# Attention in groups of four heads, with the softmax division moved to the output stage

## The reference

```
q, k, v = x@Wq.T, x@Wk.T, x@Wv.T      # 32 query heads, 8 key/value heads, 128 features per head
q, k = rope(rmsnorm(q)), rope(rmsnorm(k))
k_all = concat(k_cache[block_table], k)   # 16 pages of 32 keys = 512 cached keys, then 32 new ones
v_all = concat(v_cache[block_table], v)
scores = q @ k_all.T / sqrt(128); cached keys beyond cache_seqlens are masked
x = x + (softmax(scores) @ v_all) @ Wo.T
```

## Time and profile before

| | us |
|---|---|
| three runs | 1394.37, 1390.13, 1393.95 (median 1393.95) |
| the profiled execution | 1388.88 |
| its span in the trace | 1387.2 |
| first to last `values` product of attention (L993) | 459.9 to 1178.4 |
| last instruction of the output stage's TensorE work | about 1384 |

### The profile page before, as it was taken

One profiled execution on the slowest core, in us unless ns is written; L12 is line 12 of the kernel. 1 busy time (PEld: TensorE's weight loads), 2 busy tenths in 40 slices (PEclk: granted clock), 3 DMA queues, 4 the chain that ended last, 5 costly groups with the idle time before them and its releaser, 6 DMA issues. The chain is left out here.

```text
span 1387.2 us, 30173 instructions
## 1 busy us (share of the span) xinstructions
PE 1308.6 (94%) x8584; PEld 1134.9 (82%) x8584; DVE 924.2 (67%) x2550; ACT 750.8 (54%) x1825; POOL 743.7 (54%) x737
## 2 busy tenths in 40 slices
PE   4987999999995999999999999999999999489999
PEld 3734888888885899999999999989999998378887
DVE  4695677777764777777777777777777776432222
ACT  2074444444433677777777777767777776431121
POOL 2031999999996665656666656656566663000000
PEclk9998999999997799999999999999999999789999
DMA  9203344444338988989888988878898881643341
GB/s 302 99 32 121 79 128 125 129 132 125 80 98 222 279 246 241 255 234 263 227 263 233 252 237 244 252 222 250 241 257 232 256 235 53 238 140 115 119 130 60
DMA packets 256499, 258.26 MB, mean 186 GB/s; under 512 B 57509, under 2 KB 218021, under 8 KB 256454
## 3 DMA queue, kind: packets, MB, share of 16 engines
q1 hardware_dynamic: 246406, 232.46, 58.3%
q0 software_dynamic: 9472, 25.21, 6.6%
q10 hardware_dynamic: 576, 0.05, 0.1%
HBM read 211.49 MB, written 46.14 MB: 186 GB/s over the span
## 5 line engine op out<-in xcount | busy, mean ns | idle before, releaser
L1048 DVE CUSTOM_DVE_ANT_1 att_neg<-att_mask,att_ps 128x576 f32<-128x576 f32 x256 | 193.1, 754 | 151.8 <-PE att_ps L95 151.8
L941 POOL TENSOR_TENSOR att_k_lo<-att_kT,att_k_hi 128x544 fp32r<-128x544 f32 x128 | 173.5, 1355 | 140.8 <-ACT att_k_hi L1150 140.7
L941 POOL TENSOR_TENSOR att_k_lo<-all_room_a,att_k_hi 128x544 fp32r<-128x544 f32 x128 | 174.1, 1362 | 134.9 <-ACT att_k_hi L1150 134.9
L1135 ACT ACTIVATE att_prob<-att_neg,att_nmax 128x544 f32<-128x544 f32 x256 | 191.5, 748 | 28.9 <-DVE att_nmax L1048 6.1
L1141 ACT ACTIVATE att_pT<-att_pb 128x256 f32<-128x256 f32 x256 | 98.1, 383 | 180.5 <-PE att_pb L981 180.5
L93 PE MATMUL prj_ps<-prj_wt_hi,early_xT_lo 128*128 128x512 f32 (+1 forms) x512 | 180.2, 352 | 8.2 <-DVE prj_wt_lo L732 8.2
L93 PE MATMUL att_ps<-att_k_hi,att_q_lo 128*128 128x288 f32 (+1 forms) x512 | 171.3, 335 | 10.7 <-POOL att_k_lo L941 10.6
L94 PE MATMUL prj_ps<-prj_wt_lo,early_xT_hi 128*128 128x512 f32 (+1 forms) x512 | 174.8, 341 | 0.0
L95 PE MATMUL prj_ps<-prj_wt_hi,early_xT_hi 128*128 128x512 f32 (+1 forms) x512 | 173.2, 338 | 0.0
L94 PE MATMUL att_ps<-att_k_lo,att_q_hi 128*128 128x288 f32 (+1 forms) x512 | 149.0, 291 | 0.0
L95 PE MATMUL att_ps<-att_k_hi,att_q_hi 128*128 128x288 f32 (+1 forms) x512 | 149.0, 291 | 0.0
(11 more groups left out here) (146 smaller groups left out, 3356.0 us busy)
## 6 DMA issues: line engine op xcount, KB each, us to landing
all_room_a<-in_k_cache_t SPq DMA_DIRECT2D x256, 128.0 KB, 3.9
att_kT<-in_k_cache_t SPq DMA_DIRECT2D x256, 128.0 KB, 3.5
all_room_b<-in_L_cond_v_cache SPq DMA_DIRECT2D x160, 128.0 KB, 3.1
att_vc<-in_L_cond_v_cache SPq DMA_DIRECT2D x160, 128.0 KB, 3.1
q_scratch<-prj_qst SPq DMA_DIRECT2D x64, 256.0 KB, 2.2
o_scratch<-att_ost SPq DMA_DIRECT2D x32, 512.0 KB, 4.6
out_o_n<-o_scratch SPq DMA_DIRECT2D x32, 512.0 KB, 3.5
all_room_b<-in_L_cond_v_cache POOLq DMA_DIRECT2D x96, 128.0 KB, 3.9
```

The source lines that it names most:

```text
L941: g.tensor_tensor(k_lo[j % SPLITS][:], kT[j // HK % 2][:, :, j % HK, :], f32(k_hi[j % SPLITS][:]), ALU.subtract).then_inc(k_split, 1)
L1048: v.tensor_tensor_reduce(halves[0], halves[1], ps[j % 2][:, :, 0:KA], 1.0, 3.0e38, ALU.add, ALU.min, nmax[j % 2][:]).then_inc(maxed, 1)
L1135: act.activation(prob[j % 2][:], neg[j % 2][:, 0:KEYS], ACT.Exp, bias=nmax[j % 2][:, 0:1], scale=-1.0, accum_out=total[j % 2][:]).then_inc ...
```

## The change

- The probabilities stay undivided. The sums of 8 heads are collected in `total`, one reciprocal per batch goes into a table `inv`, which is transposed at the end of the stage and stored to `inv_d`. The output stage loads for each unit the 128 x 1024 factors it needs (`partition_broadcast` reads the same 4 KB for each of 128 partitions) and GpSimd multiplies `o_n` by them before ACT rounds it.
- The new keys' probabilities of four heads are gathered side by side (`pn`, 128 x 128), transposed in one go (`turn_new`), and copied by ACT as four diagonal blocks of 32 keys x 128 queries into a zeroed tile `pnT` (128 x 4 x 128). One float32 product of 512 columns with the dense new values `vd` (128 x 128) per group, `new_values`, takes the place of four products over 32 rows.
- `turn` does four transposes into one bank (`pt`), and DVE copies all 512 columns in one instruction (`keep`). ACT copies no more than the new keys' blocks.
- q is split four heads at a time. `valued` is raised once for four heads.
- The scratch tensors and value tiles have another order: a q load is 2 DMAs with 2 KB runs in place of one with 512 B runs, value pages come in runs of 2 KB in place of 4 KB, and `ost` is stored in 2 DMAs of 2 KB runs in place of one of 4 KB runs. The new values come in 512 B runs in place of 4 KB.

The diff, cut to its core:

```diff
...
 def load_new_keys(eng, q_d, k_d, b, q, tile, sem):
-    eng.dma_start(q[:], q_d[bass.ds(b, 1)].rearrange("a h d x -> d (a h) x")).then_inc(sem, 16)
+    for g in range(HK // GROUP):
+        h = slice(g * GROUP, (g + 1) * GROUP)
+        eng.dma_start(q[:, h, :], q_d[bass.ds(b, 1), :, h, :].rearrange("a d h x -> (a d) h x")).then_inc(sem, 16)
     eng.dma_start(tile[:, NPP].rearrange("p h t -> p (h t)"), k_d[bass.ds(b, 1)].rearrange("a d x -> (a d) x")).then_inc(sem, 16)
...
     r = slice(j % PPT * PS, (j % PPT + 1) * PS)
-    eng.dma_start(tile[r, j // PPT, :], v_pages[bass.ds(page, 1)].rearrange("a s c -> (a s) c")).then_inc(sem, 16)
+    src = v_pages[bass.ds(page, 1)].rearrange("a s (g x) -> (a s) g x", g=HK // GROUP)
+    eng.dma_start(tile[r, :, j // PPT, :], src).then_inc(sem, 16)
...
+            eng.dma_start(vd[slot][:], v_d[bass.ds(b, 1)].rearrange("a (g h) s d -> (a h s) g d", g=HK // GROUP)
+                          ).then_inc(v_in[slot], 16)
...
+                def store_out(b, slot, g):
+                    sp.wait_ge(o_staged, b * (HK // GROUP) + g + 3)
+                    cols = slice(g * GROUP * P, (g + 1) * GROUP * P)
+                    sp.dma_start(o_d[bass.ds(b, 1), :, cols].rearrange("a d x -> (a d) x"),
+                                 ost[slot][:, g * GROUP:(g + 1) * GROUP, :].rearrange("p h x -> p (h x)")
+                                 ).then_inc(o_stored[slot * (HK // GROUP) + g], 16)
...
                             load_keys(sp, b + 2, slot, pages)
+                        store_out(b, slot, 0)
+                        if not tail:
                             sp.wait_ge(valued, (b + 1) * HK)
                             load_values(sp, b + 2, slot, pages)
-                        sp.wait_ge(o_staged, (b + 1) * (HK // GROUP) + 2)
-                        sp.dma_start(o_d[bass.ds(b, 1)].rearrange("a d x -> (a d) x"),
-                                     ost[slot][:].rearrange("p h x -> p (h x)")).then_inc(o_stored[slot], 16)
+                        store_out(b, slot, 1)
...
+                for half in range(2):
+                    sp.wait_ge(inv_kept, half + 1)
+                    sp.dma_start(inv_d[half * P:(half + 1) * P, :], invT[:, half, :]).then_inc(inv_stored, 16)
+                sp.wait_ge(inv_stored, 32)
+                for i in range(UNROLL // GROUP):
+                    sp.wait_ge(o_stored[i], (B // 2 + 1) * 16)
...
+                def turn(j, bank):
+                    p = prob[j // GROUP % 2][:, j % GROUP, :]
+                    for c in range(NCH):
+                        t = pe.transpose(bank[:, c * P:(c + 1) * P], p[:, c * P:(c + 1) * P], ident[:])
+                    t.then_inc(turned, 1)
+                def turn_new(j, group, bank):
+                    pe.wait_ge(gathered, group + 1)
+                    pe.transpose(bank[:, 0:P], pn[j // GROUP % 2][:].rearrange("p h t -> p (h t)"), ident[:]).then_inc(new_turned, 1)
+                def turn_inv(half, bank):
+                    pe.wait_ge(inverted, (half + 1) * B // 2)
+                    pe.transpose(bank[:, P:2 * P], inv[:, half * P:(half + 1) * P], ident[:]).then_inc(inv_turned, 1)
...
                     s, h = j // HK % 2, j % HK
-                    cols = slice(h * D, (h + 1) * D)
+                    cols = slice(h % GROUP * D, (h % GROUP + 1) * D)
                     o = po[j // GROUP % 2][:, j % GROUP * P:(j % GROUP + 1) * P]
-                    pe.wait_ge(out_b, n + 1)
-                    for c in range(NA, NCH):
-                        pe.matmul(o, vc[s][:, c, cols], pT[j % 2][:, c, :], start=(c == NA), stop=False)
-                    pe.matmul(o, vn[s][:, cols], pT[j % 2][0:S, NCH, :], start=False, stop=False)
-                    pe.wait_ge(out_a, n + 1)
-                    for c in range(NA):
-                        t = pe.matmul(o, vc[s][:, c, cols], pT[j % 2][:, c, :], start=False, stop=(c == NA - 1))
-                    t.then_inc(valued, 1)
+                    pe.wait_ge(kept, n + 1)
+                    for c in range(NCH):
+                        pe.matmul(o, vc[s][:, h // GROUP, c, cols], pT[j % 2][:, c, :], start=(c == 0 and j % GROUP == 0), stop=False)
+                def new_values(j, group):
+                    s, g = j // HK % 2, j // GROUP % 2
+                    pe.wait_ge(new_kept, group + 1)
+                    pe.matmul(po[g][:], vd[s][:, g, :], pnT[g][:].rearrange("p h q -> p (h q)"), start=False,
+                              stop=True).then_inc(valued, GROUP)
...
                     if not (tail and j + AHEAD >= UNROLL):
                         pe.wait_ge(maxed, n + 3)
-                        scores(j + AHEAD, n + AHEAD)
-                    if not (tail and j + 2 >= UNROLL):
-                        pe.wait_ge(normed, n + 3)
-                        pe.wait_ge(out_a, n + 2)
-                        pe.wait_ge(out_b, n + 2)
-                        turn(j + 2)
+                        scores(j + AHEAD, n + AHEAD, group + 1)
+                    if j % GROUP == GROUP - 2:
+                        pe.wait_ge(kept, n + 1)
+                        turn_new(j, group, pt[new_bank_of(j)])
+                        if tail and j + 1 in INV_AT:
+                            turn_inv(INV_AT.index(j + 1), pt[new_bank_of(j)])
+                    if j % GROUP == GROUP - 1:
+                        new_values(j, group)
+                    if not late:
+                        x = j + 2
+                        pe.wait_ge(exped, n + 3)
+                        if x % GROUP == 0:
+                            pe.wait_ge(kept, n + 2)
+                        elif x % GROUP == 1:
+                            pe.wait_ge(new_kept, group + 1)
+                        else:
+                            pe.wait_ge(kept, n + 1)
+                        turn(x, pt[bank_of(x)])
...
+                    if not isinstance(group, int) or group >= 2:
+                        dve.wait_ge(scored, (group - 1) * GROUP)
+                    if g * GROUP % HK == 0:
+                        dve.wait_ge(kq_in[g * GROUP // HK % 2], (it + g * GROUP // UNROLL + 1) * 16 * KQ_LOADS)
+                    src, hi, lo = q_part(g, it)
+                    v.tensor_copy(hi[:], src).then_inc(q_hi_done, 1)
+                def split_q_lo(g, it, group):
+                    dve.wait_ge(q_hi_done, group + 1)
+                    src, hi, lo = q_part(g, it)
+                    v.tensor_tensor(lo[:], src, f32(hi[:]), ALU.subtract).then_inc(q_split, GROUP)
...
                     dve.wait_ge(scored, n + 1)
+                    if not isinstance(n, int) or n >= 2:
+                        dve.wait_ge(exped, n - 1)
...
-                def normalize(j, n):
+                def gather(j, n):
                     dve.wait_ge(exped, n + 1)
-                    v.reciprocal(inv[j % 2][:], total[j % 2][:]).then_inc(inverted, 1)
-                    dve.wait_ge(inverted, n + 1)
-                    v.tensor_scalar(prob[j % 2][:], prob[j % 2][:], inv[j % 2][:, 0:1], None, ALU.mult).then_inc(normed, 1)
+                    v.tensor_copy(pn[j // GROUP % 2][:], prob[j // GROUP % 2][:, :, L:KEYS]).then_inc(gathered, 1)
+                def invert(j, n, b):
+                    s = j // HK % 2
+                    dve.wait_ge(exped, n + 1)
+                    v.reciprocal(inv[:, bass.ds(b * HK, HK)], total[s][:]).then_inc(inverted, 1)
...
-                    dve.wait_ge(turned_a, n + 1)
-                    v.tensor_copy(pT[j % 2][:, 0:NA, :], pa[:, 0:NA * P].rearrange("p (c q) -> p c q", c=NA)).then_inc(out_a, 1)
...
+                    dve.wait_ge(turned, n + 1)
+                    v.tensor_copy(pT[j % 2][:], pt[bank_of(j)][:].rearrange("p (c q) -> p c q", c=NCH)).then_inc(kept, 1)
...
+                    n, g = it * UNROLL + j, j // GROUP + 2
+                    group = it * (UNROLL // GROUP) + g
                     if not (tail and j + 3 >= UNROLL):
                         minimum(j + 3, n + 3, it * 2 + (j + 3) // HK)
                     if not (tail and j + 1 >= UNROLL):
                         keep(j + 1, n + 1)
-                    if not (tail and j + 2 >= UNROLL):
-                        normalize(j + 2, n + 2)
-                    if not (tail and j + EARLY >= UNROLL):
-                        split_q(j + EARLY, n + EARLY, it)
+                    if not (tail and g >= UNROLL // GROUP):
+                        if j % GROUP == 0:
+                            split_q_hi(g, it, group)
+                        if j % GROUP == 2:
+                            split_q_lo(g, it, group)
+                    if j % GROUP == 1:
+                        gather(j + 2, n + 2)
+                    if j % HK == HK - 3:
+                        invert(j + 2, n + 2, it * 2 + j // HK)
...
+                def exps(j, n, b, group):
+                    s, h = j // HK % 2, j % HK
+                    if j % GROUP == 0 and (not isinstance(group, int) or group >= 2):
```

(35 more changed lines are left out.)

168 lines of the change are left out of this document (79 added, 89 removed).

## The result

| | before | after |
|---|---|---|
| median of the runs, us | 1393.54 (4 runs) | 1329.28 (4 runs, lowest 1328.01) |
| ratio, 95% interval | | 0.954 [0.952, 0.956] |
| profiled execution / span, us | 1388.88 / 1387.2 | 1328.01 / 1326.3 |
| first to last value product of attention (before L992 to L996, after L1035 to L1040) | 458.8 to 1179.2 | 461.9 to 1111.5 |
| from there to the end of the span | 208.0 | 214.8 |

One of the four runs after took 1354 us, disturbed; the comparisons leave it out. The medians gain 64 us where 79 were forecast, the profiled executions 61 where the prediction's sum has 77. Of these, attention gains 71 (86 forecast, 100 less 14). Given back are 7 behind it (9 forecast, 2 and 7) and 3 before its first value product (none forecast).

A forecast was written before the change was run, and what follows sets the result against it. TensorE bounds the kernel before, and SyncE's issuing was to set attention's pace after. Profiled 1388.9 - 100 (TensorE) + 14 (SyncE) + 2 + 7 (ends) = 1312, plus 3 for the median: 1315, range 1291 to 1348.

The forecast's parts named there:

- 100 less 14: Attention: 100 us gained by TensorE's shorter heads over 256 heads, less 14 us because SyncE sets the pace.
- TensorE's head, 2.80 to 2.41 us: Attention on TensorE: fewer transposes and no 32-row products cut each head by 0.39 us, 100 us over 256 heads.
- SyncE sets the pace at 19.9 us: Attention's DMA issues: SyncE's batch grows from 18.9 to 19.9 us, over TensorE's 19.3; price +14 us (0 to +45).
- lower bound: SyncE's batch in attention: fewer q runs free the slow key-page issues, about 1 us goes, 18.8, TensorE stays the bound.
- B: Rival, attention: SyncE has room after all, slow issues gone, the 14 us fall away, 1301; chance 0.27.
- DMA priced at 0: Attention's transfers: same 5.5 MB a batch at 276 GB/s, and halving the runs of V and o costs nothing.
- E: Rival, attention's DMA: 2 KB packets cost nearly as much as 4 KB ones, kernel 1510 at 0.17 us each; chance 0.04.
- C: Rival: crowding, DMA engines (full at 280 GB/s) or the output stage's loop bind, about 1340; chance 0.17.
- The covers: Attention: DVE, ACT and POOL stay under TensorE's head, and new waits for copies and valued are priced at 0.
- The output stage: Steady units stay at 5.44 us; factor load and 2.56 us multiplication are hidden with 0.7 us to spare.
- The ends: Attention's last group +2 us; output stage's first units +7 us (3 to 12) for unhidden multiplications and loads.
- D: Rival, TensorE around L993: long steps are waits for pT, not the 32 rows; about 1378; chance 0.05.

The follow-up runs named there:

- e4_before_128: Kernel before, with the product of the 32 new values run over all 128 rows, the added rows zeroed once: 1328.14 us, ratio 0.958.
- g4_pairs: Kernel after, with GpSimd issuing its six value pages in pairs at three heads instead of one at each of six: 1329.33 us, ratio 0.958.
- f1_act_stores: Kernel after, with the two stores of ost per batch issued by ACT's queue instead of SyncE: 1332.84 us, ratio 0.960.
- f3_two_pages_less: f1_act_stores without two of SyncE's ten value pages per batch from the third batch on: 1330.37 us, ratio 0.958.
- e1_v_one_run: Kernel after, with value pages and their tile back in one run of 4 KB per partition: 1321.47 us, ratio 0.951.
- g1_act_pairs: f1_act_stores with GpSimd's six value pages issued in pairs at three heads: 1302.26 us, ratio 0.938.
- g3_less_pairs: f3_two_pages_less with GpSimd's six value pages issued in pairs at three heads: 1287.77 us, ratio 0.926.
- e5_no_factor_load: Kernel after, without the output stage's broadcast load of inv, GpSimd's multiplication kept: 1331.05 us, ratio 0.958.
- g2_one_run_pairs: Kernel after, with value pages in one 4 KB run, ost stores issued by ACT and GpSimd's value pages in pairs: 1298.45 us, ratio 0.933.
- e2_pool_8: Kernel after, with eight value pages per batch issued by GpSimd instead of six: 1445.46 us, ratio 1.041.
- e3_before_v2: Kernel before, with value pages and tiles in two runs of 2 KB: 1402.25 us, ratio 1.009.

## Why the prediction was right, and where it was off

- **TensorE's head, 2.80 to 2.41 us.** Right in kind: the cost sat around the product of 32 rows, e4_before_128 shows it alone. Slightly too dear in size: where nothing else limits, the batch is 18.7 us, 2.34 a head, since eight value passes take 0.81 us instead of 0.88. The Trainium skill (TensorEngine Tiling (Array Packing), Key Properties) says that a change of tiling mode drains TensorE; the trace agrees for the product over 32 rows (0.38 us a head, around and in it) and shows none for the transpose to 32 columns, whose steps stay at 0.11 us in e4_before_128 too.
- **SyncE sets the pace at 19.9 us.** The mechanism was right: its waits fell to 2.6 us. The term was mis-sized. The added q load and store cost 0.34 and 0.40 us and 0.30 of register work, 1.04 where 1.0 was reckoned. The step that failed is the one that changed the runs of V and priced only the packets: the issue of a value page grew from 0.37 to 0.57 us, 2.0 us a batch, which the prediction did not have. Cheaper key pages (0.8) and page numbers (0.7) gave 1.5 back, and new k 0.2. The prediction's lower bound had the gain in the key pages, but with another reason: the long issues went with the 4 KB value pages, not with q's runs. The page numbers it did not have at all. The result is 20.3 instead of 19.9. That it came so near is luck in part, since the two terms that were missed nearly cancel. Over the 29 looped batches the measured 20.46 is 16 us more than 19.9, which is the 15 us that attention missed.
- **The wait that was not seen.** The prediction names no wait for GpSimd's pages. But one page per head is a date counted in heads: with shorter heads the last one leaves 3.7 us before TensorE's need in place of 5.0, and in the denser traffic it lands after 4.7 us in place of 3.5. Each of the two takes about half of what was lost. The margin of 1.5 us before was in the trace. In the kernel after this costs nothing beyond SyncE's 20.3 (g4_pairs), but it would have kept B, "SyncE has room, 1301", from coming true: f1_act_stores gave SyncE its room and stayed at 1332.84. B needed both.
- **DMA priced at 0.** Right up to this pace: share 0.92 at 270 GB/s, and f3_two_pages_less gains nothing. E is refuted, as after moves 270 GB/s at 0.92 and e1_v_one_run with 4 KB packets 272 at 0.96; a 2 KB packet takes 0.107 us on the mean between 600 and 1050 us, under the 0.12 that the prediction set as E's sign. C's figure for full engines, 280 GB/s, is met by g1_act_pairs at 283; this limit shows only once the other two are gone.
- **The covers.** The new waits that were priced at 0 cost next to nothing: in g3_less_pairs, which has them all, TensorE is idle for 3.4 of 450 us. DVE's copy of 512 columns takes 687 ns (forecast 0.70), GpSimd's multiplication 2415 ns (2.56):

```profile
L1155 DVE COPY att_pT<-att_pt 128x512 f32<-128x512 f32 x256 | 175.8, 687 | 25.1 <-PE att_pt L1016 25.1
...
L1404 POOL TENSOR_TENSOR out_o_n<-out_o_n,all_room_b 128x1024 f32<-128x1024 f32 x32 | 77.3, 2415 | 138.0 <-DMA all_room_b<-inv_scratch 138.0
```

- **The output stage.** TensorE's step stays at 5.44 us a unit (26 of 28 steps within 0.03 us, the other two 5.57 and 5.70), and the factor's load is hidden (e5_no_factor_load). The page's DMA issues (KB each, us from issue to landing):

```profile
out_o_n<-o_scratch SPq DMA_DIRECT2D x32, 512.0 KB, 3.4
all_room_b<-inv_scratch SPq DMA_DIRECT2D x32, 512.0 KB, 5.5
```

  The second load lands 5.5 us after its issue where the sum has 4.7 (3.4 + 1.3), so by that sum nearly nothing of the 0.7 us to spare is left. The two longer steps fit that, and so do ACT's starts, which came every 5.4 to 5.5 us before and now vary from 4.6 to 6.4. The ends cost 7 us where 9 were forecast. The 3 us before attention's first value product were in no term; for 1.9 us of them TensorE stands idle until a value page has landed (0.3 before).
- **D** is refuted by e4_before_128.

## What to carry to other kernels

When a bound engine is made faster, list every piece of work that is scheduled by counting its steps, and compare lead time with latency anew: a load issued n steps ahead has fewer microseconds ahead of it afterwards, and if the traffic grows denser it may also take longer to land. When two resources end at nearly the same pace, removing either shows nothing; test them together before calling one innocent. The cost of a DMA for the engine that issues it depends on its access pattern, so a change of runs has to be priced on the queue as well as in the packets.

## What the runs showed of the hardware

- **Issue time by shape.** A load of 128 KB into 32 partitions takes SyncE 0.37 us with one run per partition (before, e1_v_one_run, g2_one_run_pairs; 244 to 285 GB/s) and 0.57 with two (e2_pool_8, e3_before_v2, after, g1_act_pairs; 230 to 283 GB/s). These are medians.
- **4 KB runs hold the issuing engine up.** With value pages of 4 KB 16 key pages take 6.7 to 7.4 us a batch, and between 600 and 1050 us 11 to 35 issues are over 0.7 us, the longest 1.6 (e4_before_128); with 2 KB the pages take 6.3 to 6.4 us and none or one issue is over 0.7 us (the longest 1.25, g4_pairs). The traffic is not the reason: g2_one_run_pairs (4 KB) and g1_act_pairs (2 KB) move 285 and 283 GB/s.
- **Reading the page numbers.** The 16 numbers that SyncE reads into registers take 2.0 to 2.1 us behind a store of 512 KB that it issued (before, e3_before_v2, e4_before_128), 1.4 to 1.5 behind one of 256 KB (after, e1_v_one_run, e2_pool_8, g4_pairs), and 1.0 where ACT issues the stores.
- **DVE and GpSimd stand in each other's way.** In g4_pairs DVE's rounding of q takes 0.42 us at best and 2.65 us where GpSimd has two instructions back to back behind its pair of DMAs (start us, us):

```profile
820.53 2.65 DVE L1123 CAST att_q_hi<-all_q 128x512 fp32r<-128x512 f32 x1
```

```profile
819.14 1.08 POOL L543 DMA_DIRECT2D all_room_b<-in_L_cond_v_cache  x2
820.25 2.64 POOL L975 TENSOR_TENSOR att_k_lo<-all_room_a,att_k_hi 128x544 fp32r<-128x544 f32 x2
```

DVE's instruction begins 0.3 us after GpSimd's first and ends 0.3 after its second. DVE's busy time in 450 us rises from 320.7 to 370.6 us with as many instructions. The Trainium skill (SBUF — State Buffer, SBUF: two separate sides) describes a port pair shared by the two, which whichever starts first holds for its whole instruction while the other is blocked. The trace agrees, with a delay that here lasts over two instructions of the other engine; no run shows that it is this port. It cost nothing here, where SyncE set the pace. In g3_less_pairs, with the same pairs, DVE is busy for 396.6 of 450 us and TensorE for 446.6; whether it costs g1_act_pairs something was not tried.
- **Granted clock.** In the kernel after TensorE idles for 29 of 450 us, in pieces of at most 2.7 us, and the mean clock stays at 0.99: twice it is 1.2 GHz for 3.4 us. In e2_pool_8 TensorE idles for 3.6 us on the mean (at most 3.9) at the start of each of 19 batches, has 1.2 GHz for 3.4 us each time, and the mean is 0.93.
